# Edge attributes and their weights padded with zero rows from 5 to 128 contraction rows, in a kernel of two graph layers

## What is computed

```python
def mesh_conv(x, src, dst, ea, w1, b1, g, bt, w2, b2):
    m = jnp.concatenate([x[dst], x[src], ea], axis=-1) @ w1 + b1
    m = jax.nn.silu(group_norm(m, g, bt)) @ w2 + b2
    out = jax.ops.segment_sum(m, dst, num_segments=n)
    return out / jnp.clip(cnt, 1.0)[:, None]
...
logits = (q[dst] * k[src]).sum(-1) * scale + (edge_attr @ ew + eb)
w = softmax over the edges of each destination
o = segment_sum(w[:, :, None] * v[src], dst)
```

## Time and profile before

| what | value |
|---|---|
| median of three runs | 15801.92 us (15791.97 to 15820.28) |
| span of the profiled execution, first to last instruction | 12412.9 us |
| time of the profiled execution beyond the span | not given with the profile |
| mean granted clock of PE | 0.816 of 2.4 GHz |
| PE busy | 10184.1 us, 82% of the span |
| GpSimd busy | 6565.9 us, 53% |

### The profile page before, as it was taken

One profiled execution on the slowest core, in us unless ns is written; L12 is line 12 of the kernel. 1 busy time (PEld: TensorE's weight loads), 2 busy tenths in 40 slices (PEclk: granted clock), 3 DMA queues, 4 the chain that ended last, 5 costly groups with the idle time before them and its releaser, 6 DMA issues. The chain is left out here.

```text
span 12412.9 us, 238807 instructions
## 1 busy us (share of the span) xinstructions
PE 10184.1 (82%) x52788; PEld 7837.8 (63%) x52788; DVE 6784.3 (55%) x13638; ACT 4227.0 (34%) x19321; POOL 6565.9 (53%) x6535
## 2 busy tenths in 40 slices
PE   0018999999999949999999569999996489999994
PEld 0015666666666637777777457777775378888882
DVE  0024555555555447777777546666665545555555
ACT  0003434433343404444344113333332045555552
POOL 0005444444444317777677237777774077777770
PEclk9996666666666658988898669999998589999996
DMA  1013222222222214444444246666663255555652
GB/s 17 14 48 88 83 82 83 82 82 82 82 84 81 65 58 118 123 121 121 116 121 119 72 118 178 180 178 178 180 178 106 57 130 134 136 136 134 134 135 74
DMA packets 1697918, 1336.67 MB, mean 108 GB/s; under 512 B 595131, under 2 KB 1473914, under 8 KB 1695443
## 3 DMA queue, kind: packets, MB, share of 16 engines
q1 hardware_dynamic: 1462376, 792.32, 23.6%
q0 software_dynamic: 234784, 537.91, 16.7%
HBM read 1255.24 MB, written 74.14 MB: 107 GB/s over the span
## 5 line engine op out<-in xcount | busy, mean ns | idle before, releaser
L452 POOL DMA_INDIRECT conv_gath<-b,conv_idx x3232 | 3262.3, 1009 | 3529.4 <-issue 1893.1
L830 POOL DMA_INDIRECT gat_gath<-g,gat_idx x1616 | 1606.2, 994 | 941.6 <-issue 495.5
L830 POOL DMA_INDIRECT attn_gath<-kv,attn_idx x1616 | 1642.8, 1017 | 847.0 <-issue 517.7
L476 PEld LDWEIGHTS conv_z<-conv_win,conv_hotT 128*128 128x128 f32 x6464 | 1226.0, 222 | 934.1 <-issue 705.0
L478 PE MATMUL conv_z<-wc,conv_ea 5*128 5x128 f32 x6464 | 1799.4, 363 | 0.0
L476 PE MATMUL conv_z<-conv_win,conv_hotT 128*128 128x128 f32 x6464 | 1719.6, 353 | 0.0
L594 DVE TENSOR_REDUCE conv_var<-conv_sq 128x32 f32<-128x512 f32 x808 | 551.7, 683 | 1891.1 <-ACT conv_sq L524 1891.0
L478 PEld LDWEIGHTS conv_z<-wc,conv_ea 5*128 5x128 f32 x6464 | 1100.8, 212 | 470.7 <-issue 173.1
L493 PE MATMUL conv_sums<-conv_hot,conv_m 128*128 128x128 f32 x6464 | 1319.2, 372 | 8.3 <-ACT conv_m L556 7.8
L493 PEld LDWEIGHTS conv_sums<-conv_hot,conv_m 128*128 128x128 f32 x6464 | 1138.8, 267 | 201.6 <-issue 167.5
L469 PE MATMUL conv_z<-conv_gath,ident 128*128 128x512 f32 x1616 | 1173.7, 818 | 58.8 <-DMA conv_gath<-b,conv_idx 58.7
(11 more groups left out here) (338 smaller groups left out, 17743.5 us busy)
## 6 DMA issues: line engine op xcount, KB each, us to landing
conv_win<-a SPq DMA_DIRECT2D x3232, 64.0 KB
conv_places<-places SPq DMA_DIRECT2D x202, 512.0 KB
attn_win<-q SPq DMA_DIRECT2D x1616, 64.0 KB
gat_xeT<-in_xeT SPq DMA_DIRECT2D x404, 256.0 KB
conv_gath<-b,conv_idx POOLq DMA_INDIRECT x3232
attn_places<-places SPq DMA_DIRECT2D x101, 512.0 KB
gat_places<-places SPq DMA_DIRECT2D x404, 128.0 KB
attn_gath<-kv,attn_idx POOLq DMA_INDIRECT x1616
```

The costliest lines, as they stand in the source:

```text
L452: pool.indirect_dma_start(gath[:, b.c * BQ + k, t, :], None, b_table, bass.IndirectOffsetOnAxis(ap=idx[:, b.c, k * QT + t:k * QT + t + 1], ...
L476: nc.tensor.matmul(zt, hotT[:, s6, t * P:(t + 1) * P], win[:, s4, t, :], start=False, stop=False, skip_group_check=True)
L830: pool.indirect_dma_start(gath[:, b.c * BQ + k, t, :], None, table, bass.IndirectOffsetOnAxis(ap=idx[:, b.c, k * QT + t:k * QT + t + 1], a ...
```

## The change

The buffer `ea`, the weights `wc1`, `wc2` (L478) and `we` (L864) get 128 partitions in place of 5. Their rows from 5 on are zero: DVE clears the weights before the first loads of the program, and clears the three places of `ea` at the head of both convolutions and of attention; SP waits for these clears. The transfers still write 5 rows. The products at L478 and L864 then contract over 128 rows, as those at L476 and L862 do.

```diff
@@ prepare
         @block.sync
         def _(sp):
+            sp.wait_ge(padded, 3)
             for dst, src in loads:
                 sp.dma_start(dst, src).then_inc(loaded, 16)
@@
         @block.vector
         def _(dve):
+            for name in ("wc1", "wc2", "we"):
+                nc.vector.memset(C[name][:, :], 0.0).then_inc(padded, 1)
             link = Chain(dve, chain)
@@
-                centred += [(... (C[f"wc{l}"][:, :], ED + 1, 1),
+                centred += [(... (C[f"wc{l}"][:, :], P, 1),
@@ conv_edges (and, where gat is false, attention_edges)
-        ea = st.sb("ea", [ED + 1, RB, BE])
+        ea = st.sb("ea", [P, RB, BE])
@@
-                                 (ea[:, b.c, :], w["ea"][:, bass.ds(b.i * BE, BE)]),
+                                 (ea[0:ED + 1, b.c, :], w["ea"][:, bass.ds(b.i * BE, BE)]),
@@
-            sp.wait_ge(zeroed, 1)
+            sp.wait_ge(zeroed, 2)
@@
+            nc.vector.memset(ea[:, :, :], 0.0).then_inc(zeroed, 1)
             nc.vector.memset(zero[:, :], 0.0).then_inc(zeroed, 1)
@@ build
-             ... "we": sb("we", [ED + 1, H0]),
+             ... "we": sb("we", [P, H0]),
@@
-            ... C[f"wc{l}"] ... = ... sb(f"wc{l}", [ED + 1, P]) ...
+            ... C[f"wc{l}"] ... = ... sb(f"wc{l}", [P, P]) ...
```

More of the change, by code:

```diff
@@ L201, in prepare @@
         wt_ready = st.sem("wt_ready")
+        padded = st.sem("padded")
         loads = [(dst_b[:, :], w["dst_b"]), (dst_r[:, :], w["dst_r"]), (n0_b[:, :], w["n0_b"]),
@@ L322, in _ @@
             for l in (1, 2):
-                centred += [(C[f"wab{l}"][:, :, :].rearrange("p a f -> p (a f)"), P, 2), (C[f"wc{l}"][:, :], ED + 1, 1),
+                centred += [(C[f"wab{l}"][:, :, :].rearrange("p a f -> p (a f)"), P, 2), (C[f"wc{l}"][:, :], P, 1),
                             (C[f"w2{l}"][:, :], P, 1), (row(C, f"c{l}_b2"), P, 1)]
@@ L789, in fetch @@
                                  D["places"][bass.ds(b.i, 1), :].to_broadcast([P, BE])).then_inc(places_landed[b.c], 16)
-                    sp.dma_start(ea[:, b.c, :], w["ea"][:, bass.ds(b.i * BE, BE)]).then_inc(places_landed[b.c], 16)
+                    sp.dma_start(ea[0:ED + 1, b.c, :], w["ea"][:, bass.ds(b.i * BE, BE)]).then_inc(places_landed[b.c], 16)
                 for k in range(BQ):
@@ L817, in _ @@
             early(Batch(0, 0))
-            sp.wait_ge(zeroed, 1)
+            sp.wait_ge(zeroed, 1 if gat else 2)
             run_batches(sp, fetch)
@@ L983, in _ @@
                 dve.sem_inc(s, HEAD)
+            if not gat:
+                nc.vector.memset(ea[:, :, :], 0.0).then_inc(zeroed, 1)
             nc.vector.memset(zero[:, :], 0.0).then_inc(zeroed, 1)
@@ L1573, in build @@
              "expand": sb("expand", [P, 3, P]), "te": sb("te", [P, P]), "rows": sb("rows", [P, len(ROWS), P]),
-             "wq": sb("wq", [P, P]), "wkv": sb("wkv", [P, 2, P]), "wo": sb("wo", [P, P]), "we": sb("we", [ED + 1, H0]),
+             "wq": sb("wq", [P, P]), "wkv": sb("wkv", [P, 2, P]), "wo": sb("wo", [P, P]), "we": sb("we", [P, H0]),
              "wsd": sb("wsd", [P, 2, P]), "weta": sb("weta", [P, P + NS]), "ones_b": sb("ones_b", [P, 1], BF16), "wsa": sb("wsa", [P, 3 * H1])}
         for l in (1, 2):
-            C[f"wab{l}"], C[f"wc{l}"], C[f"w2{l}"] = sb(f"wab{l}", [P, 2, P]), sb(f"wc{l}", [ED + 1, P]), sb(f"w2{l}", [P, P])
+            C[f"wab{l}"], C[f"wc{l}"], C[f"w2{l}"] = sb(f"wab{l}", [P, 2, P]), sb(f"wc{l}", [P, P]), sb(f"w2{l}", [P, P])
         cnt = sb("cnt", [P, 2, NBLK])
```

## The result

The changed kernel takes 15,428.29 us (median of 4 runs, 15,418.23 to 15,444.24), the kernel before 15,797.19 in the same comparison (15,791.97 to 15,820.28): ratio 0.9756, 95% interval 0.9738 to 0.9775. It is faster by 369 us where 1,172 were forecast (15,802 to 14,630); the time lies above the range of 13,400 to 15,100.

The account below looks back on a forecast made before the run. PE was taken to bound both convolutions, with the gathers as floor in all edge stages. Gains of 1088 and 102 us less 20 for clears gave -1170 us, 14,630 us with the constant; range 13,400 to 15,100.

Parts of the forecast that it names:

- From the span to the time: Whole kernel: the 3389 us between profiled span and median time carried as a constant, giving 14,630 us.
- The pace: L476/L478 in the convolutions: equal row extents take an instruction from 0.201 us to 0.125 at the high clock.
- The clock: PE in both convolutions: denser streaming with all rows keeps the clock high nearly throughout, above 0.9, from 0.66 and 0.89.
- Convolution 1: Edge stage: from 2.073 to 1.40 us a gather over 1616 gathers, 1088 us gained.
- both hitches: Convolution 1, each batch: ScalarE begins L553 3.86 us late, PE stands 1.95 us before the counts; 1162 gained if hidden.
- the gathers' 21.7 us: Edge stages: GpSimd's gathers set a floor of 21.7 us a batch, 1.354 us a gather, that no PE work lowers.
- Convolution 2: Edge stage: from 1.417 us a gather to the gathers' 1.354 over 1616 gathers, 102 us gained.
- Clears and heads: Buffer clears at three stage heads and weight clears before the first loads: 20 us added, with the handovers.
- Attention's zero: Attention: PE's quad shortens by up to 0.9 us, all behind the gathers, so 0 gained.
- pace alone: Rival, 7 in 100: zero rows don't count for the clock, convolution 1 gains 350 us, convolution 2 nothing; 15,470 us.
- Another limit: Rival, 4 in 100: gathers are slower in timed executions, so convolution 1 soon meets them; 15,600 us.
- theory C: From the experiments: GpSimd's index lists cause the late instructions; plain transfers in the changed kernel give below 9,500 us.

Follow-up runs that it names:

- before_again: The kernel before, unchanged, profiled once more: 15,838.53 us.
- grouped: The kernel before (5 rows), with each convolution quad issuing its four L476 products first, then its four L478 products: 15,257.66 us, ratio 0.9752.
- rows32: The changed kernel with the L478 products over 32 rows instead of 128, attention still padded to 128: 15,648.08 us, ratio 0.9988 to the kernel before.
- after_again: The changed kernel itself, run once more, on a chip of the first kind: 11,021.93 us, ratio 0.8818 to the kernel before.
- no_ea_again: The kernel before without the L478 products of edge attributes in both convolutions, on a chip of the first kind: 11,129.63 us, ratio 0.8903.
- plain_before: The kernel before with plain transfers of 128 consecutive fixed rows in place of all gathers: 12,536.03 us, ratio 1.0029.
- plain_after: The changed kernel with plain transfers of 128 consecutive fixed rows in place of all gathers: 10,023.09 us, ratio 0.8021 to the kernel before.
- fixed_both: The changed kernel with SyncE's window loads and ScalarE's copies at fixed rows instead of node-number rows: 14,733.02 us, ratio 0.9407 to the kernel before.
- fixed_sp: The changed kernel with only SyncE's window loads at fixed rows, ScalarE unchanged: 11,031.2 us, ratio 0.8826 to the kernel before.

## Why the prediction was wrong, by its own steps

**From the span to the time: the step that failed.** "I carry them as a constant" was called the weakest step by the prediction itself, and it was. The 3389 us were not outside the span: the profile shown had been taken in an execution of 12,413 us, the timed ones were of 15,800 us, and on the chips of that kind every stage is longer (before_again against the shown profile: +423, +972, +871 and +1151 us). The forecast was a sum over a profile of one kind of chip, put on the time of the other, where the same change gains 369 us.

**The pace: right, on both kinds.** 0.11 us an instruction against 0.125 taken and 0.115 as the lower end. `grouped` shows the cause as the prediction had it, a change of row extent between neighbours, and `rows32` that 32 rows against 128 pace as slowly as 5. That load and product queue up at such a change was the prediction's picture of it; the runs show the pace only. The rule that I weighed, of the Trainium skill, page "TensorE: Matmul & The Clock Gate", section "Part 3: Packing small matmuls" (loads overlap only where row groups differ), does not agree with these traces: products with the same 128 rows go at 0.11 us, those with unlike extents at 0.20, and in `after_again` loads (1274.05 us) and products (1658.83) of one window of 2000 us must overlap. The same section also lets a load go ahead into the background weight buffer, which the traces don't contradict; the rule was weighed without that.

**The clock: right where the stages reach the gathers.** 0.95 in both convolutions of after_again, above the 0.9 named. In convolution 1 it is 0.90 with 5 rows, grouped, and 0.69 with 32 rows, alternating, so the low clock there goes with the alternation and not with the count of rows. Why isn't shown, and slow, unbroken streaming alone is not enough: in the kernel before, convolution 2 has the same alternation with PE never idle at 0.89, attention alternates too at 0.97, and there padding goes with 0.89. `no_ea_again`, without any 5-row product in the convolutions, has 0.87 and 0.85. On chips of the second kind it is 0.76 and 0.74 after the change, where PE is idle for over a third of the time.

**The sum on the kind of chip that it was made from.** Convolution 1: -1179 (forecast -1088; the 16 instructions lose 1.43 us a quad at the high level, 3.22 to 1.79, and not 1.22, so PE's batch with both hitches comes to the gathers' 21.7 us and not to 22.4; the hitch before the counts is still there, 202.0 us in 104 times). Convolution 2: -169 (-102; a gather goes at 1.32, not 1.354). Attention: -73 (0). GAT: 0 (0). Clears and heads: +30 (+20). Together -1391 where -1170 was forecast; by medians on one chip -1487. The profile of before is thus 76 and 96 us shorter than the medians on the two chips of the first kind; which chip it came from is unknown.

**Attention's zero was wrong, and so was its reason.** "Two stages of quite different products have one pace: the gather queue." `plain_before`, without gathers, has attention at 2290 us and GAT at 2205, `plain_after` 1785 and 2207: both stages of before were held by PE, which the earlier trace rows show 97% and 95% busy beside GpSimd's 99%. GAT's 1.354 lay near the gathers' pace by chance. The "370 us" named for attention without gathers measured 505. The conclusion for the convolutions held nonetheless, by luck in this step, since the gathers' own floor turned out at 1.32 to 1.34.

**Where 1,172 became 369.** On chips of the second kind the change takes about as much busy time off PE (11,899.0 to 9487.7 us) as on those of the first (10,184.1 to 7834.3), but not the late instructions. In convolution 1 PE's work filled 87% of the window before, and the stage took 3796 us, 423 more than in the shown profile. After the change it fills 61%, and the stage takes 3471 where `after_again` has 2194. What grew is idle time of PE that nothing in the profile ends, most of it before the counts; here from before_again, the changed kernel and `after_again`, in the bounds of the stage:

```profile
PE conv_counts L488 <- issue: 282.0, 123, 8.0
PE conv_counts L492 <- issue: 772.7, 206, 15.0
PE conv_counts L492 <- issue: 202.0, 104, 2.0
```

Summed over PE's lines "issue" is 448, 1286 and 202 us. I read this as lateness that had lain beside PE's own work and is left bare without it; no run on these chips takes the lateness away alone. Convolution 2 gains 72 us, with PE 88% busy at a clock of 0.69 before and 63% at 0.74 after; which chain holds it there is not shown. Of the rivals, "pace alone" (7 in 100, 15,470 us) comes nearest to the time, by luck: its convolution 1 was 3020 us and not 3471, and its low clock had another reason. "Another limit" (4 in 100, 15,600 us) is nearest in substance, for a cause that it did not have: the gathers are not slower (0.99 us), they wait for their tables.

**Open:** what makes single instructions of PE, SyncE and ScalarE come late on those chips. In the changed kernel's trace 93% of SyncE's begin during a gather or in the 0.32 us behind one. Such time is 63% of the four stages, and of SyncE's short instructions of the same kinds 34% begin in it, so gathers and late instructions go together; but chips of the first kind gather as well. PE's late starts come mostly 0.7, 1.4 or 2.1 us behind the one before (935, 678 and 328 of them), which is one, two or three times the 0.7 us of SyncE's and ScalarE's. `fixed_both` cut 3.5% there and `fixed_sp` nothing on the first kind (11,031 against 11,022 us, each on its own chip). The plain transfers, which would test theory C, were not run on a chip of the second kind.

## What to carry to other kernels

Compare a profile's span with the timed median before anything else; in every execution here with both on record they lie within 3 us of each other. If they differ by more, the profile may be of another kind of execution, and its idle times and bounds not those of the timed one: forecast both kinds. Here products of unlike contraction extents that alternated cost 0.09 us an instruction more at the high clock, where one with 128 columns otherwise took 0.11; order such products in groups, or give them equal extents. A common pace of two stages isn't proof of a common bound: where two engines are near 100% busy, take one's work away to tell them apart.

## What the runs showed of the hardware

- One kernel, two kinds of chip: the kernel before takes 12,489 and 12,509 us on two, 15,669 and 15,852 on two others, each within 1% over its runs. The profiles differ in late instructions of PE, SyncE and ScalarE, those of the last two of 0.7 us, and in the granted clock (0.816 against 0.711); VectorE and GpSimd are busy about as long (6784.3 and 6565.9 us against 6759.2 and 6412.1).
- The price of alternating row extents is the same on both kinds: 0.200 to 0.213 us against 0.112 an instruction at 2.4 GHz, 0.347 to 0.375 against 0.214 at 1.2 GHz (medians over all of a run). One change slows two starts.
- An indirect gather occupies GpSimd for 1.01 us and a plain transfer of 128 rows for 0.55, yet on the kernel before this changes next to nothing (ratio 1.0029, on a chip of the first kind): there PE is the bound in every edge stage.
